# A gated cross-attention and feed-forward network on one core: the fusing stage and the last feed-forward stage as one pipeline

## The chip, the core and the metric

The kernel runs on one core of a Trainium2 chip. The time is that of the device, in microseconds (us), from launch to end, as the median of several executions. The core has five engines that run their own instruction lists: TensorE (PE, matrix products into the eight PSUM banks; its weight loads are shown apart as PEld), VectorE (DVE), ScalarE (ACT), GpSimd (POOL) and SyncE (SP, which here only issues transfers). They meet at semaphores. An engine executes its list in order, so whatever stands behind a wait waits too.

## The reference

The input `x` has 8 batches of 512 tokens with 512 values. Four layers follow one another, each added to `x` with a gate: attention over a context of 77 tokens, a mixture of experts (each token goes to its best two of eight, and to two shared ones), attention over the same context without projections, and a quantised feed-forward network with a convolution along the tokens. Only the last two and the end of the second concern us:

```python
routed_out = einsum('etd,te->td', routed, gates)          # two experts a token
x = x + tanh(g_ffn[0]) * (routed_out + shared_out)
# layer 3
h = layernorm(x)
p = softmax(h @ ctx.T)                                     # 77 scores a token
x = x + tanh(g_xattn[1]) * (p @ ctx)
# layer 4
h = layernorm(x)
h = quant(h) @ quant(w1).T                                 # 512 -> 2048, int8 per token
h = silu(conv3(h along the tokens) + conv_b)
x = x + tanh(g_ffn[1]) * (quant(h) @ quant(w2).T)          # 2048 -> 512
```

`quant` of an activation takes the largest absolute value of each token, scales to 127 and rounds.

## The kernel before

`flamingo` calls four stages: `attention`, `experts`, `fuse` and `ffn`. Each is a block of its own: no engine starts the next one before all have ended the last. The first two are not touched. A token tile is 128 tokens; a batch is four of them.

`fuse` (L1360) takes one batch a step, with three batches under way (`front`, `mid`, `back`). SP loads the residual rows `x2`; POOL gathers the two expert rows of each token by indirect transfers (L1517), eight a batch. DVE adds them with their gates (L1606, L1613) and takes the statistics (L1589, L1595), POOL the reciprocal root (L1525), ScalarE normalises (L1580). TensorE transposes (L1684), computes the scores (L1691), transposes the probabilities (L1695) and multiplies with the context (L1701); ScalarE copies and takes exponentials (L1568), DVE adds the result (L1661) and takes statistics again (L1666). The last third normalises (L1563), takes row maxima (L1633), quantises (L1576) and dequantises (L1601). The rows `x3` and `xd` go to DRAM (L1494, L1499). POOL loads the 4 MB `w1q` and the 2 MB `w2q` while this runs (L1532, L1533). The steady steps are a hardware loop.

`ffn` (L1706) loads `xd` and `x3` again. Its step also has three batches under way. TensorE transposes `xd` (L2033), ScalarE and DVE keep the result as a high and a low half (L1871, L1917). Then come the 16 up-projection tiles of 128 hidden values (L1988, eight matmuls each) through a ring of three PSUM banks `f_ps`. For each tile ScalarE writes the middle tap of the convolution into `h` (L1854), DVE adds the outer two (L1890, L1893), ScalarE applies the silu (L1836). DVE takes the maxima of eight tiles at a time (L1901), TensorE transposes them (L1998), DVE computes the token scales (L1906 to L1913), TensorE spreads them (L2004), ScalarE copies the row `srow` (L1847). For the batch before, POOL multiplies each tile with it (L1826; DVE does this for the last batch, L1936) and ScalarE rounds ("lifts") two tiles in each of slots 6 to 13 (L1841). For the batch before that, TensorE runs the down-projection one token tile at a time, sixteen matmuls and one for the offset (L1963, L1965): two token tiles at the start of the step, one behind up tile 5, one behind up tile 11. DVE adds the result to `x3` (L1883), and it goes out (L1803). `h` has three buffers. The last down-projection (L1976) runs through four banks at once, part by part behind the liftings.

## Time and profile before

| | |
|---|---|
| median of 3 runs | 1919.27 us (1912.75 to 1922.49) |
| profiled execution, its own time | 1918.68 us |
| its span, first to last instruction | 1917.2 us |
| mean granted TensorE clock | 0.904 |
| PE busy | 1653.6 us (86%), 8636 instructions |
| DVE busy | 1137.7 us (59%), 1946 instructions |
| ACT busy | 794.9 us (41%), 1417 instructions |
| POOL busy | 588.0 us (31%), 541 instructions |

Busy is the share of the span in which an engine executes something; waits, branches and the issuing of transfers don't count. The shares are averages over stages that differ. The activity strip cuts the span in 40 slices of 48 us and gives each a digit in tenths. `fuse` is slices 26 to 30, where PE drops to 3 to 7 and its clock to 5 to 7; `ffn` is the rest:

```profile
PE   7599999999866999998999999837674889999997
DVE  3587878878745344532223333258875777777775
ACT  2243433434313422222334443325563556566653
POOL 0133323333212444464331000065513243344440
PEclk9798989889967999999999999957666899999999
```

### The profile page before, as it was taken

How to read it: one execution, taken by the hardware profiler on the slowest of the kernel's cores; microseconds unless marked ns; L12 is line 12 of the kernel's file. 1: busy time of each engine (PE TensorE's matmuls, PEld its weight loads, DVE VectorE, ACT ScalarE, POOL GpSimd, SP SyncE). 2: the span in 40 equal slices, each digit the busy share in tenths (PEclk: the TensorE clock that was granted, in tenths of full speed). 3: DMA queues.
4: the chain of work that ended last, by engine and by line, in shares of the span. 5: the costliest groups of instructions: out<-in, count | busy, mean ns of one | idle time of the engine just before them, and what ended most of it. 6: DMA issues, size and time to landing. Idle time of an engine off the chain costs nothing. (4 is left out here: it accounts for less than half of the span.)

```text
span 1917.2 us, 26044 instructions
## 1 busy us (share of the span) xinstructions
PE 1653.6 (86%) x8636; PEld 1304.5 (68%) x8636; DVE 1137.7 (59%) x1946; ACT 794.9 (41%) x1417; POOL 588.0 (31%) x541
## 2 busy tenths in 40 slices
PE   7599999999866999998999999837674889999997
PEld 5578888788745888886778888624343666666664
DVE  3587878878745344532223333258875777777775
ACT  2243433434313422222334443325563556566653
POOL 0133323333212444464331000065513243344440
PEclk9798989889967999999999999957666899999999
DMA  3112122121129889984443333287743111111102
GB/s 124 44 45 88 55 77 88 44 88 55 67 74 351 286 304 316 321 282 138 162 139 107 107 108 106 94 303 287 256 148 110 44 44 66 66 66 38 51 23 88
DMA packets 108196, 252.02 MB, mean 131 GB/s; under 512 B 15027, under 2 KB 15027, under 8 KB 103912
## 3 DMA queue, kind: packets, MB, share of 16 engines
q1 hardware_dynamic: 65272, 121.98, 19.0%
q0 software_dynamic: 17056, 67.12, 9.7%
q10 hardware_dynamic: 25808, 62.14, 9.2%
q8 instruction: 35, 0.57, 0.1%
q14 instruction: 25, 0.20, 0.0%
HBM read 147.13 MB, written 101.97 MB: 130 GB/s over the span
## 5 line engine op out<-in xcount | busy, mean ns | idle before, releaser
L1275 PE MATMUL e_u_ps<-e_w,e_xeT 128*128 128x512 f32 x1596 | 393.1, 398 | 10.8 <-DVE e_xeT L1180 10.8
L1275 PEld LDWEIGHTS e_u_ps<-e_w,e_xeT 128*128 128x128 f32 x1596 | 293.1, 189 | 73.3 <-DVE e_w L1229 8.9
L1988 PE MATMUL b_f_ps<-b_xdT,w1q 128*128 128x512 f32 x1024 | 254.1, 404 | 11.5 <-DVE b_h L1893 9.4
L1988 PEld LDWEIGHTS b_f_ps<-b_xdT,w1q 128*128 128x128 f32 x1024 | 191.4, 190 | 64.8 <-DVE b_h L1893 18.3
L1826 POOL TENSOR_TENSOR b_h<-b_h,b_srow 128x512 f32<-128x512 f32 x112 | 143.6, 1342 | 245.9 <-ACT b_srow L1847 245.9
L1286 PE MATMUL e_y_ps<-e_w,e_hT 128*128 128x512 f32 x798 | 209.9, 405 | 4.3 <-DVE e_hT L1211 2.8
L1286 PEld LDWEIGHTS e_y_ps<-e_w,e_hT 128*128 128x128 f32 x798 | 143.3, 190 | 31.0 <-issue 4.0
L1854 ACT ACTIVATE b_h<-b_f_ps,cb,cw 128x512 f32<-128x512 f32 x128 | 104.2, 814 | 124.5 <-PE b_f_ps L1988 124.3
L1890 DVE SCALAR_TENSOR_TENSOR b_h<-b_f_ps,cw,b_h 128x511 f32<-128x511 f32 x128 | 95.9, 749 | 85.9 <-ACT b_h L1854 85.7
L490 ACT ACTIVATE pT<-t_ps 77x512 f32<-77x512 f32 x128 | 71.9, 590 | 119.0 <-PE t_ps L691 119.0
L465 POOL TENSOR_TENSOR prob<-prob,ri 128x1232 f32<-128x1232 f32 x32 | 74.9, 2341 | 115.3 <-DVE ri L572 115.3
L1211 DVE TENSOR_TENSOR e_hT<-e_h_ps,e_hT 128x256 fp32r<-128x256 f32 x69 | 29.3, 424 | 134.8 <-ACT e_hT L1046 134.8
L1965 PE MATMUL b_o_ps<-w2q,b_h 128*128 128x512 bf16 x448 | 106.2, 392 | 0.0
L730 PE MATMUL m_ps<-wo,oT 128*128 128x512 f32 x384 | 96.3, 407 | 7.1 <-DVE oT L598 7.0
L744 PE MATMUL m_ps<-xT,wq 128*128 128x256 f32 x768 | 98.3, 289 | 1.4 <-DVE xT L554 1.4
L1836 ACT ACTIVATE b_h<-b_h 128x512 f32<-128x512 f32 x128 | 86.7, 677 | 30.8 <-DVE b_h L1893 30.8
L1893 DVE SCALAR_TENSOR_TENSOR b_h<-b_f_ps,cw,b_h 128x511 f32<-128x511 f32 x128 | 96.2, 752 | 4.5
L691 PE MATMUL t_ps<-ident,prob 128*77 128x128 f32 x512 | 90.8, 340 | 7.6 <-ACT pT L490 4.9
L744 PEld LDWEIGHTS m_ps<-xT,wq 128*128 128x128 f32 x768 | 95.4, 196 | 1.8 <-DVE xT L554 1.8
L442 POOL TENSOR_TENSOR ve<-mv,eps 128x2 f32<-128x2 f32 x32 | 6.2, 194 | 289.6 <-DVE mv L583 289.6
L730 PEld LDWEIGHTS m_ps<-wo,oT 128*128 128x128 f32 x384 | 73.0, 194 | 27.9 <-DVE oT L598 11.5
L985 POOL DMA_INDIRECT slots_in_scratch<-e_srow,e_scol x64 | 71.8, 1122 | 56.7 <-DMA e_srow<-xn_scratch 37.3
(221 smaller groups left out, 2869.1 us busy)
## 6 DMA issues: line engine op xcount, KB each, us to landing
e_xe<-slots_in_scratch SPq DMA_DIRECT2D x69, 256.0 KB, 2.6
experts_out_scratch<-e_ye ACTq DMA_DIRECT2D x69, 256.0 KB, 2.0
xin<-in_x SPq DMA_DIRECT2D x16, 512.0 KB, 3.8
xres<-in_x SPq DMA_DIRECT2D x16, 512.0 KB, 4.5
x_scratch<-x SPq DMA_DIRECT2D x32, 256.0 KB, 2.1
xn_scratch<-xn SPq DMA_DIRECT2D x32, 256.0 KB, 2.1
e_xe<-xn_scratch SPq DMA_DIRECT2D x32, 256.0 KB, 4.2
e_fraw<-in_w1T ACTq DMA_DIRECT2D x8, 1024.0 KB, 8.3
```

Of the source, the lines that this page charges most:

```text
L691: mm = pe.transpose(t_ps[0:C, t[("p", j, g)] % 2, i * P:(i + 1) * P], prob[:, j, g * HG + i, :], ident[:])
L730: mm = pe.matmul(m_ps[:, m[f"w{j}"] % 2], oT[:, pa, k, j * P:(j + 1) * P], wo[:, pb, k, :], start=(k == 0 and (pa, pb) == PASSES[0]), stop ...
L744: mm = pe.matmul(m_ps[:, m[f"q{i}"] % 2, g * W2:(g + 1) * W2], wq[:, pa, k, mt * P:(mt + 1) * P], xT[:, pb, k, :], start=(k == 0 and (pa, ...
L1275: mm = pe.matmul(u_ps[:, i], xeT[:, pa, k], w[:, par, pb, k * 2 * HID:(k + 1) * 2 * HID], start=(k == 0 and (pa, pb) == PASSES[0]), stop=( ...
L1286: mm = pe.matmul(y_ps[:], hT[:, pa, i * KH + k], w[:, par, pb, W1N + k * D:W1N + (k + 1) * D], start=(i == 0 and k == 0 and (pa, pb) == PA ...
L1826: pool.tensor_tensor(ht, ht, srow[:], ALU.mult).then_inc(u_done, 1)
L1836: act.activation(ht, ht, ACT.Silu).then_inc(h_done, 1)
L1854: act.activation(tile(s, m), f_ps[:, (s * KF + m) % RING], ACT.Identity, bias=cb[:, m:m + 1], scale=cw[:, m, 1:2]).then_inc(mid_tap, 1)
L1890: dve.scalar_tensor_tensor(out=ht[:, 1:S], in0=f[:, 0:S - 1], scalar=cw[:, m, 0:1], in1=ht[:, 1:S], op0=ALU.mult, op1=ALU.add).then_inc(pr ...
L1893: dve.scalar_tensor_tensor(out=ht[:, 0:S - 1], in0=f[:, 1:S], scalar=cw[:, m, 2:3], in1=ht[:, 0:S - 1], op0=ALU.mult, op1=ALU.add).then_in ...
L1965: mm = pe.matmul(o_ps[:, j % 2], rounded(s - 2, k, j), w2q[:, k, :], start=False, stop=(k == KF - 1))
L1988: mm = pe.matmul(f_ps[:, u % RING], w1q[:, k, m * P:(m + 1) * P], xdT[:, part, k], start=(k == 0 and part == 0), stop=(k == KD - 1 and par ...
```

## The change

`fuse` and `ffn` become one block, `tail`, whose steps run over `s` from -2 to 9, each written out as slots `m` = 0 to 15. In step `s` the expert rows of batch `s+2` are combined (`comb_next`), batch `s+1` goes through cross-attention and quantising (`cross`), batch `s` through the up-projection (`up`), the hidden values of batch `s-1` get their token scales (`quant`), and batch `s-2` goes through the down-projection (`down`). There is no hardware loop.

- `x3` and `xd` no longer go through DRAM; the rows of a batch stay in one of five buffers `X` from load to output.
- ScalarE multiplies the gathered rows with their gates (`gate_experts`, slots 1, 2, 9, 10) and POOL adds them, where DVE did both. The gathers take their indices straight from `slot`; `y` has four row buffers, and each pair of gathers is issued behind the additions that free its buffers.
- The down-projection works on all four token tiles at once, in four banks of its own (`y_ps`): part `m` follows up tile `m` in each slot. DVE's four outputs come together at the end of the step.
- Everything else on TensorE shares one ring of four banks, `r_ps`, in written order (`ring`): up tiles, transposes, scores, probabilities, maxima, scale row, attention. A use waits for the last reader of the use four before it.
- `h` has two buffers instead of three; a middle tap waits for the down-projection part that frees its tile (`h_free`). ScalarE lifts one tile a slot: tiles 7 to 15 of batch `s-2` in slots 0 to 8, tiles 0 to 6 of batch `s-1` in slots 9 to 15.
- `w1q` is loaded behind the first four gathers, `w2q` on SP's queue.

```diff
-        n.w1q = keep("w1q", [P, KD, DH], FR)
...
-        fuse(nc, n)
-        ffn(nc, n)
+        tail(nc, n)
...
+        r_ps = psum("r_ps", [P, RING, 512])
+        y_ps = psum("y_ps", [P, TB, D])
...
+            for s in range(-2, B + 2):
+                run(s, 0 <= s - 2, 0 <= s - 1 < B, 0 <= s < B, 0 <= s + 1 < B, s + 2 < B)
+
+        ring = []
+        for s in range(-2, B + 1):
+            for m in range(KF):
+                if 0 <= s < B:
+                    ring.append(("f", s, m))
+                if 0 <= s + 1 < B:
+                    if m < 2:
+                        ring += [("x", s + 1, 2 * m), ("x", s + 1, 2 * m + 1)]
+                    if m == 2:
+                        ring.append(("s", s + 1, 0))
+                    if m == 4:
+                        ring.append(("p", s + 1, 0))
+                if 1 <= s <= B:
+                    if m == 4:
+                        ring += [("a", s - 1, 0), ("a", s - 1, 1)]
+                    if m == 6:
+                        ring.append(("r", s - 1, 0))
+                if 0 <= s + 1 < B and m in (7, 8):
+                    ring += [("o", s + 1, 2 * m - 14), ("o", s + 1, 2 * m - 13)]
+            if 0 <= s + 1 < B:
+                ring += [("d", s + 1, j) for j in range(TB)]
...
@@ GpSimd, one step @@
+                if 2 <= s <= B:
+                    products(s - 2, 7, KF)
+                if comb_next:
+                    combine(s + 2, 0)
+                    combine(s + 2, 1)
+                if quant and up:
+                    pool.wait_ge(row_done, s)
+                    products(s - 1, 0, 2)
+                if cross:
+                    rstd(1, mv2_done, s + 1, nmr2_done)
+                if quant and up:
+                    products(s - 1, 2, 4)
+                if comb_next:
+                    combine(s + 2, 2)
+                    combine(s + 2, 3)
+                if quant and up:
+                    products(s - 1, 4, 7)
+                if comb_next:
+                    rstd(0, mv1_done, s + 2, nmr1_done)
...
@@ ScalarE, in slot m @@
+                    if up:
+                        if s >= HB:
+                            act.wait_ge(h_free, (s - HB) * KF + m + 1)
                         act.wait_ge(f_full, s * KF + m + 1)
...
+                    if 2 <= s <= B and m < 9:
+                        lift_tile(s - 2, 7 + m)
+                    if quant and up and m >= 9:
+                        lift_tile(s - 1, m - 9)
+                    if comb_next and m in (1, 2, 9, 10):
+                        gate_experts(m - 1 if m < 3 else m - 7)
...
@@ VectorE, in slot m and behind the slots @@
+                    if up:
                         taps(m)
...
+                    if quant and m == 5:
+                        token_scales()
+                    if cross and m in (8, 9):
+                        fused(2 * m - 16)
+                        fused(2 * m - 15)
+                    if cross and m == 9:
+                        aggregate(1, stats[0] - TB, mv2_done)
+                    if up and m == 10:
+                        half_max(0)
...
+                if quant and not up:
                     dve.wait_ge(row_done, s)
                     for m in range(KF):
...
                         dve.tensor_tensor(ht, ht, srow[:], ALU.mult).then_inc(u_done, 1)
...
+                if down and not up:
+                    for j in range(TB):
+                        outputs(j)
...
@@ TensorE, in slot m @@
+                    if up:
+                        up_tile(m)
+                    if down and m >= 1:
+                        down_part(m)
+                    if cross and m < 2:
+                        normed_transposes(2 * m)
+                        normed_transposes(2 * m + 1)
+                    if down and m == 0:
+                        down_part(0)
+                    if cross and m == 2:
+                        scores(0)
+                        scores(1)
+                    if cross and m == 4:
+                        prob_transposes()
+                    if quant and m == 4:
+                        max_transposes(0)
+                        max_transposes(1)
+                    if quant and m == 6:
+                        scale_row()
+                    if cross and m in (7, 8):
+                        attend(2 * m - 14)
+                        attend(2 * m - 13)
+                if cross:
+                    for j in range(TB):
+                        quantised_transposes(j)
```

## Rows read from the trace of the kernel before

**Rows 1.** Windows: stretch, its length, busy us of PE, PEld, DVE, ACT, POOL, clock, DMA.
```profile
1244.40:1457.80 213.40, 121.20 (x480) 78.00 (x480) 155.88 (x368) 101.26 (x201) 88.39 (x111) 0.63 0.68 238
1457.80:1469.80 12.00, 3.67 (x16) 3.27 (x16) 2.76 (x4) 2.39 (x4) 11.92 (x3) 0.54 0.32 91
...
1877.40:1917.20 39.80, 29.56 (x136) 15.88 (x134) 21.36 (x30) 11.09 (x18) 0.00 (x0) 0.90 0.22 79
```

**Rows 2.** Chain that ended last, up tiles 2 to 5 of two batches: start, us, what.
```profile
1675.65 7.47 PE b_f_ps L1988 x32
...
1838.65 7.46 PE b_f_ps L1988 x32
```

**Rows 3.** Timeline of `ffn`: start, us, engine, line, operation, tiles, count, idle before.
```profile
1670.80 3.96 PE L1988 MATMUL b_f_ps<-b_xdT,w1q 128*128 128x512 f32 x16
...
1672.99 0.80 ACT L1854 ACTIVATE b_h<-b_f_ps,cb,cw 128x512 f32<-128x512 f32 x1 [10.30 <-PE b_f_ps L1988]
...
1675.38 7.30 PEld L1988 LDWEIGHTS b_f_ps<-b_xdT,w1q 128*128 128x128 f32 x32
...
1682.97 3.35 PEld L1965 LDWEIGHTS b_o_ps<-w2q,b_h 128*128 128x128 f16 x16
```

**Rows 4.** Timeline of `ffn`, ScalarE and DVE at slots 7 to 9.
```profile
1688.70 0.82 ACT L1854 ACTIVATE b_h<-b_f_ps,cb,cw 128x512 f32<-128x512 f32 x1 [4.14 <-PE b_f_ps L1988]
1689.55 0.76 DVE L1890 SCALAR_TENSOR_TENSOR b_h<-b_f_ps,cw,b_h 128x511 f32<-128x511 f32 x1 [4.00 <-ACT b_h L1854]
...
1691.13 0.80 ACT L1854 ACTIVATE b_h<-b_f_ps,cb,cw 128x512 f32<-128x512 f32 x1
...
1698.21 4.41 DVE L1901 TENSOR_REDUCE b_am<-b_h 128x512 f32<-128x4096 f32 x1
```

**Rows 5.** POOL: the products in the timeline, the gathers in the groups by line.
```profile
1679.47 20.53 POOL L1826 TENSOR_TENSOR b_h<-b_h,b_srow 128x512 f32<-128x512 f32 x16 [34.23 <-ACT b_srow L1847]
...
L1517 POOL DMA_INDIRECT y<-experts_out_scratch,ycol x64 | 64.0, 999 | 23.7 <-issue 16.7 <-POOL ycol L1513 6.7 <-DVE f_mv L1595 0.3
```

**Rows 6.** Groups by line in `fuse`: busy us, mean ns of one, idle before.
```profile
L1701 PE MATMUL f_o_ps<-f_craw,prT 77*128 77x512 f32 x64 | 57.0, 1071 | 5.5 <-ACT prT L1571 5.5
L1691 PE MATMUL f_s_ps<-f_ctraw,f_xT 128*128 128x77 f32 x256 | 30.9, 281 | 0.0
```

**Rows 7.** Timeline of `fuse`, the first batches and the last.
```profile
1270.52 0.16 DVE L1649 SCALAR_TENSOR_TENSOR nmr<-f_mv,f_rs 128x4 f32<-128x4 f32 x1 [1.45 <-POOL f_rs L1525]
...
1276.86 1.28 ACT L1568 ACT_TABLE_LOAD   x1
...
1291.86 0.41 DVE L1595 BATCH_NORM_AGGREGATE f_mv<-f_st 128x2 f32<-128x6 f32 x4
...
1295.77 2.93 ACT L1563 ACTIVATE xq<-x,nmr,f_rs 128x512 f32<-128x512 f32 x4 [1.14 <-DVE nmr L1626]
...
1298.22 2.45 DVE L1633 TENSOR_REDUCE am<-xq 128x1 f32<-128x512 f32 x4
...
1304.76 2.54 ACT L1576 ACTIVATE xq<-xq,sc 128x512 f32<-128x512 f32 x4
...
1445.65 2.93 ACT L1563 ACTIVATE xq<-x,nmr,f_rs 128x512 f32<-128x512 f32 x4 [8.51 <-DVE nmr L1626]
```

**Rows 8.** Transfers of `fuse`: issues, KB each, median us to landing.
```profile
w1q<-w1q_scratch POOLq DMA_DIRECT2D x1, 4096.0 KB, 15.1
...
y<-experts_out_scratch,ycol POOLq DMA_INDIRECT x64, 6.3
```

**Rows 9.** Timeline of the end: DVE's products for the last batch.
```profile
1888.35 2.50 DVE L1936 TENSOR_TENSOR b_h<-b_h,b_srow 128x512 f32<-128x512 f32 x4 [2.79 <-ACT b_srow L1847]
```

**Rows 10.** Windows in `ffn`, as rows 1: TensorE's clock around two pauses.
```profile
1508.00:1512.00 4.00, 0.45 (x2) 0.45 (x3) 4.00 (x2) 0.00 (x0) 0.00 (x0) 0.50 0.93 284
1512.00:1516.00 4.00, 4.00 (x14) 3.27 (x13) 3.06 (x8) 0.00 (x0) 0.00 (x0) 0.50 0.64 241
...
1660.00:1662.00 2.00, 2.00 (x12) 1.94 (x11) 1.21 (x2) 1.84 (x4) 0.00 (x0) 0.52 0.00 0
```

More of the change, by code:

```diff
@@ L1933, in run @@
+                if comb_next:
+                    combined(2)
+                    combined(3)
+                    aggregate(0, stats[0] - TB, mv1_done)
+                if cross:
+                    for j in range(TB):
+                        low(j)
+                if down and up:
+                    for j in range(TB):
+                        outputs(j)
+                if up:
+                    half_max(1)
+                if quant and not up:
                     dve.wait_ge(row_done, s)
@@ L2040 @@
+                if cross:
+                    for j in range(TB):
+                        quantised_transposes(j)
+            whole(run)
 def kernel(x, ctx_1024, g_xattn, g_ffn, L0_xattn_Wq, L0_xattn_bq, L0_xattn_Wk, L0_xattn_bk, L0_xattn_Wv,
```

848 lines of the change are left out of this document (359 added, 489 removed).

## Prediction, made before the changed kernel ran

> **What bounds the kernel now.** I read the activity strip of the page first, then windows by stage, then the timeline inside the last two stages. The change touches only what comes after the expert stage, from 1244.4 us on. There the fusing stage takes 213.4 us with TensorE granted 0.63 of its clock and busy 121 us; DVE, at 156 us, is its busiest engine [rows 1]. A hand-over of 12.0 us follows (a block boundary, the first load of `xd`, its transposes), then the feed-forward stage, and 39.8 us from its last convolution to the end [rows 1]. In the steady feed-forward stage one batch takes (1838.65 - 1675.65)/3 = 54.3 us [rows 2]. A batch of the fusing stage takes about 22 us (from 1295.77, the second normalisation of the first batch, to that of the eighth at 1445.65 it is 7 x 21.4 [rows 7]). So a batch costs some 76 us in both stages together.
>
> In the feed-forward stage TensorE is the bound. An up-projection tile is eight matmuls at 0.229 us from start to start (7.30 us for 32), 1.8 us; a down-projection matmul is 0.213 us (3.35 us for 16) [rows 3]. One batch is 16 x 1.8 + 68 x 0.213 = 43.5 us, and with 16 + 16 transpose-like instructions and the four sets of `xd` transposes about 48 of the 54.3 us. The first matmul of a tile starts at 1670.80 and ScalarE's reading of it at 1672.99: 2.2 us, that is 0.4 us behind the last matmul [rows 3].
>
> **The prices of the other engines.** Between two middle taps ScalarE does a silu and two liftings, four instructions in 1691.13 - 1688.70 = 2.43 us, about 0.6 us each. A tile's two outer taps are 2 x 0.76 = 1.5 us of DVE, and half of a batch's maximum 4.4 us [rows 4]. A product on POOL is 20.53/16 = 1.28 us, a gather 80.7/64 = 1.26 us (busy and issue) [rows 5]. Four normalisations are 2.9 us, four quantisations 2.5 us, four row maxima 2.5 us [rows 7].
>
> **The sum of one full slot sequence (batches 2 to 5), engine by engine.**
> - TensorE: 48 us as above, plus 16 transposes (2.7 us), scores (32 instructions of about 0.1 us, 3.2), transposes of the probabilities (0.6) and attention. An attention instruction runs 0.89 us (57.0/64) at a clock of 0.63, about 0.45 us at the full one, and a batch has 8 of them: 3.6 us [rows 6]. Together 58 us.
> - DVE: 16 x 1.5 + 2 x 4.4 + outputs 2.8 + low halves 2.5 + token scales 2.1 + attention's four outputs with their statistics 5.8 + statistics of the combined rows 2.5 + row maxima 2.5 + dequantising 1.7 + some small ones 2.5 = 55 us. The two combining passes have left DVE.
> - ScalarE: 48 tile instructions at about 0.6 (30), two normalisations (5.8), quantising (2.5), eight gatings (4.9), eight copies (4.3), exponentials (1.3), and two table loads of 1.28 each, because each batch now has its exponentials between silus (the trace has the load where the first exponential follows the experts' silus [rows 7]): 52 us.
> - POOL: 16 products (20.5), 8 additions for combining (10.3, priced as products), 8 gathers (10), two reciprocal roots (3.6): 44 us.
>
> No engine needs more than 58 us. If only the busiest counted, the stage would shrink from 76 to some 60 us a batch. I don't forecast that, because all three engines must pass each tile on in turn through one ring of four PSUM banks, which now carries the cross-attention's tiles too.
>
> **The wait structure, slot by slot.** Time 0 is the end of DVE's last taps of the step before. "Mid m" is the start of ScalarE's middle tap of tile m; it now waits for the down-projection part that frees the buffer (two `h` buffers, not three): tile start + 1.8 + 0.86 + 0.4 = 3.1 us.
> - Boundary: low halves end at 4.2, outputs at 7.0, the second maximum at 11.3; down part 0 waits for the outputs. Mid 0 at 9.5, taps 0 from 11.3 to 12.8. The third transpose set waits for taps 0. Mid 1 is at 12.2, mid 2 at 17.1.
> - Scores stand ahead of tile 3 on TensorE: mid 3 at 23.0. Table load, exponentials, a lifting: mid 4 at 27.4; second load, silu.
> - Tile 5 takes the bank of tile 4 (three maxima and probability banks lie between): it starts when taps 4 end at 29.7, mid 5 at 32.8. Tile 6 takes the bank of the probabilities (copied at 34.6): mid 6 at 37.6. Tile 7 stands behind the scale row, which waits for token scales behind taps 5: mid 7 at 41.4. Tile 8 takes the scale row's bank (43.2): mid 8 at 46.2.
> - Attention output 3 and tile 9 wait for DVE's fused rows 0 and 1 (49.2, 50.6): mid 9 at 53.6. Taps 9, fused rows 2 and 3, aggregate: 59.1.
> - Then DVE: taps 10, maximum, taps 11, statistics, taps 12, row maxima and scales until 72.1.
> - POOL starts its root at 59.1: 1.8, products 2 and 3 (2.6), two combinings with two gathers behind each (2 x 5.4), product 4: 75.6. ScalarE's lifting of that tile stands ahead of quantising, which thus runs 76.2 to 78.6 and not 72.1 to 74.6. Mid 14 at 78.6, taps 14, dequantising, taps 15 end at 84.
>
> So 84 us a full step, against 76: each slot from 4 to 9 is a chain over three engines of 4 to 7 us.
>
> **The sum.** From 1244.4. The first batch's rows are ready at 1270.5 now [rows 7]. In the new order the 4 MB load of `w1q` is issued behind the first four gathers and ahead of the next four, on the same queue; it took 15.1 us to land [rows 8]. If the gathers wait for it the rows are ready at 1285, if not at 1278; I take 1281. Cross-attention of batch 0, nothing beside it: now 1270.5 to 1292.3 for the fused rows and statistics [rows 7], then root, normalisation, maxima, quantising, dequantising, transposes, copies, 11 us: 33 us, 1314. Step 0 (no down-projection, no products): the same chain, 61 us, 1375. Step 1 (no outputs, no down parts): 84 - 9 = 75, 1450. Steps 2 to 5: 4 x 84 = 336, 1786. Step 6 (nothing to combine, quantising at once): 78, 1864. Step 7 (no cross-attention): taps 0 at 11.3, then TensorE, 16 x 2.7: 53, 1917. The end: outputs and maximum 7.1, transposes, scales and row 5.8, 16 products at 0.625 (2.50 for 4 [rows 9]) 10, then DVE's outputs of batch 6 (2.8), and only behind them the whole down-projection of batch 7, 68 x 0.213 = 14.7, outputs 2.8 and the last transfer 4.8: 48, against 39.8 now [rows 1]. Today that down-projection runs beside the liftings. 1965, and with the 1.5 us between span (1917.2) and time (1918.68): 1966. The profiled execution is 0.6 us under the median.
>
> **Two prices weighed.** A switch of ScalarE's table is 1.28 us in the trace [rows 7], and I use that. The Trainium skill (ScalarE: Activation LUTs, What ACT_TABLE_LOAD costs) adds a drain and puts a switch at 2.66 us; by that figure a full step would be an estimated 2.8 us longer and the time 1984 us. No row here shows such a drain.
>
> TensorE's clock: with TensorE nearly idle from 1508 to 1512 the granted clock is 0.50, the lower level of 1.2 GHz, and it stays there from 1512 to 1516 with TensorE busy all 4.00 us; behind the pause from 1656 on it is 0.52 in 1660 to 1662 [rows 10]. By my schedule TensorE idles some 10 us in each full step, from the last down part to the dequantised rows, so tile 0 takes 3.6 us, not 1.8, and taps 0 start about 1 us later, since DVE's maximum covers the rest. I price it at 0 to 1 us a step (in the 84). The Trainium skill (TensorE: Matmul & The Clock Gate, HAM oscillation) says that matmul groups separated by idle time keep falling back to half rate; the row agrees, and this is the third rival's mechanism.
>
> **Rivals.**
> 1. Faster: the overlap works and the busiest engine bounds. Today's feed-forward step is 54.3 for 48 us of its bound, 1.13; 58 x 1.13 = 65. Then steps 2 to 5 lose 19 us each, 0, 1 and 6 some 32 in all: 1966 - 108 = 1858. For it: no engine is over 58 us, and two stages' idle time lies open to each other. Against it: bank and order waits above. It decides from 77 us a full step: seven steps of cross-attention at 7 us less win back the 47 us. Between (about 77): 1919.
> 2. Late gathers: from issue to landing a gather takes 6.3 us [rows 8]; POOL issues those of the next pair only behind each combining. Should a pair land after ScalarE reaches slot 9, gating waits with the tiles of slots 9 and 10 behind it, about 3 us a step: 1966 + 6 x 3 = 1984. Against it: by my times 14 us or more lie between issue and gating.
> 3. Slower still: the clock stays at its lower level through slots 3 to 9, where TensorE works in pieces of 2.7 us between waits. Six tiles and their down parts at double time, less what is hidden: 6 to 8 us a step for six steps: 2005 to 2010. Against it: in those slots my pauses are 1 to 3 us, shorter than the two above behind which the clock fell.
>
> **How the numbers follow.** A measurement tells 0.5% (10 us) from no change. Forecast, steps of 79 to 88 us: 0.44, between 1940 and 1990. Rival 2: 0.06. Rival 3: 0.12. Rival 1: 0.26. Between, steps near 77: 0.12, of which 0.05 faster, 0.07 same. Faster 0.31, same 0.07, slower 0.62. The range 1880 to 2005 leaves out most of rival 1 and the far end of rival 3; the forecast's own range is 1940 to 1990.
>
> **What would show it.** Full steps of 84 us from one table load pair to the next; DVE idle for ScalarE in slots 3 to 9; ScalarE waiting for POOL's product ahead of quantising; TensorE's tile 5 and 9 released by DVE; 16 table loads; a last down-projection that starts only behind DVE's outputs. If DVE or TensorE is busy over 80% between 1450 and 1786, the forecast is wrong, and if the steps are under 77 us its sign is.

## The result, and the profile after

The changed kernel takes 2014.37 us (1999.44 to 2017.20), the kernel before, in the same comparison, 1920.05 us: 1.048 times as long, interval 1.042 to 1.054. The forecast was 1966 us, its range 1880 to 2005. The sign was right, the size was not.

The profiled execution has a span of 2011.9 us (1917.2 before) at a mean clock of 0.895 (0.904). The first part of the page after; the activity strip is in 40 slices of 50 us:

```profile
PE 1665.0 (83%) x8636; PEld 1308.7 (65%) x8636; DVE 1101.6 (55%) x1874; ACT 850.9 (42%) x1495; POOL 669.3 (33%) x628
...
PE   7599999999849999999999996266676878787796
...
PEclk9798898898769999999999998578888979797899
...
HBM read 130.36 MB, written 85.20 MB: 107 GB/s over the span
```

Against the kernel before, VectorE has 36 us less to do, ScalarE 56 and GpSimd 81 us more, as the change moved it, and 33.5 MB of transfers are gone (147.13 MB read and 101.97 written before). Yet PE is at 6 to 8 tenths from the first up tile on, but for one 9 near the end, where the old feed-forward stage had 8s and 9s. Windows of the kernel after (length; busy us of PE, PEld, DVE, ACT, POOL; clock), which answer to [rows 1]: the start, steps 1 to 3, and from the last taps to the end:

```profile
1244.40:1325.00 80.60, 19.10 (x76) 13.34 (x76) 21.76 (x46) 26.43 (x46) 45.01 (x49) 0.54 0.54 187
1385.00:1465.00 80.00, 52.99 (x220) 39.65 (x220) 50.85 (x81) 46.53 (x79) 30.32 (x31) 0.80 0.15 43
1465.00:1556.40 91.40, 69.19 (x300) 47.27 (x300) 53.72 (x87) 53.74 (x92) 41.80 (x40) 0.85 0.10 27
1556.40:1645.50 89.10, 67.24 (x289) 45.70 (x288) 53.45 (x85) 52.49 (x89) 41.77 (x40) 0.84 0.17 51
...
1961.70:2011.90 50.20, 34.92 (x152) 17.58 (x152) 24.30 (x37) 15.96 (x27) 0.00 (x0) 0.90 0.17 63
```

DVE's 53, ACT's 53 and POOL's 42 us a step are close to the forecast's 55, 52 and 44. TensorE's 67 to 69 are not its 58, since it ran at 0.85 of its clock. The step is 20 us longer than that.

The forecast's terms against the trace, a step counted from one last tap of DVE to the next:

| term | forecast | measured | difference |
|---|---|---|---|
| first up tile starts | 1314 | 1326.3 | +12.3 |
| step 0 | 61 | 61.4 | +0.4 |
| step 1 | 75 | 80.1 | +5.1 |
| steps 2 to 5 | 336 | 88.5 + 89.1 + 88.5 + 84.9 = 351.0 | +15.0 |
| step 6 | 78 | 86.2 | +8.2 |
| step 7 (no cross-attention) | 53 | 57.0 | +4.0 |
| the end | 48 | 49.9 | +1.9 |

Together 46.9 us, which is the whole miss of the profiled execution. Step 3 on TensorE (start, us, what; in brackets the idle time before and its releaser):

```profile
1560.29 3.78 PE L1914 MATMUL t_r_ps<-t_xdT,t_w1q 128*128 128x512 f32 x8 [2.71 <-DVE t_xdT L1816]
...
1586.97 2.13 PE L1914 MATMUL t_r_ps<-t_xdT,t_w1q 128*128 128x512 f32 x8 [1.29 <-DVE t_h L1774]
...
1591.89 3.23 PE L1914 MATMUL t_r_ps<-t_xdT,t_w1q 128*128 128x512 f32 x8 [1.90 <-ACT t_prT L1702]
1594.93 1.56 PE L1897 MATMUL t_y_ps<-t_w2q,t_h 128*128 128x512 bf16 x4
...
1597.13 2.10 PE L1914 MATMUL t_r_ps<-t_xdT,t_w1q 128*128 128x512 f32 x8
...
1608.30 1.10 PE L1962 MATMUL t_r_ps<-t_craw,t_prT 77*128 77x512 f32 x2 [2.36 <-DVE t_x L1790]
1609.58 3.69 PE L1914 MATMUL t_r_ps<-t_xdT,t_w1q 128*128 128x512 f32 x8 [0.19 <-DVE t_x L1790]
...
1642.88 3.38 PE L1968 MATMUL t_r_ps<-ident,t_xw 128*128 128x128 f32 x14 [11.49 <-DVE t_xw L1850]
```

Tile 5 waits for the taps of tile 4, tile 6 for the copy of the probabilities, tile 9 stands behind the attention output that waits for DVE's fused row: the bank waits as forecast. Not forecast is the length of tiles 6 and 9: 3.2 and 3.7 us, where tile 7 takes 2.1. Windows of the same stretch:

```profile
1590.00:1592.00 2.00, 0.11 (x1) 0.11 (x1) 1.02 (x2) 1.97 (x4) 0.00 (x0) 1.00 0.00 0
1592.00:1594.00 2.00, 2.00 (x6) 1.60 (x7) 1.93 (x5) 0.44 (x1) 0.00 (x0) 0.64 0.01 4
1594.00:1596.00 2.00, 2.00 (x6) 0.80 (x5) 0.45 (x4) 0.00 (x0) 0.00 (x0) 0.51 0.00 0
1596.00:1598.00 2.00, 2.00 (x15) 1.74 (x13) 0.63 (x1) 1.48 (x3) 0.00 (x0) 1.00 0.01 4
...
1610.00:1612.00 2.00, 2.00 (x6) 1.52 (x6) 0.26 (x1) 0.00 (x0) 0.00 (x0) 0.50 0.65 159
```

The granted clock went to its lower level (1.2 GHz) behind pauses of 1.90 and 2.36 us, and came back some 3 us later. Both falls stand in each of steps 2 to 6. The forecast had argued that pauses of 1 to 3 us would not do this.

The trace of the kernel before already had such a fall, at the start of a feed-forward step (TensorE, then the window; the clock had been 1.00 from 1712 to 1714):

```profile
1712.98 0.66 PE L2033 MATMUL b_f_ps<-ident,b_xd 128*128 128x128 f32 x4 [2.18 <-DVE b_h L1893]
1714.42 1.76 PE L2033 MATMUL b_f_ps<-ident,b_xd 128*128 128x128 f32 x8 [0.79 <-DVE b_h L1893]
...
1716.00:1718.00 2.00, 2.00 (x6) 0.74 (x5) 2.00 (x2) 1.01 (x3) 0.00 (x0) 0.50 0.36 38
```

Nor does the length of a pause alone tell. In step 0 of the changed kernel pauses of 2.24 and 2.35 us brought no fall (1.00 from 1342 to 1348 and from 1355 to 1361). e6_lock, a kernel of the experiments below, is the same program as the changed one up to step 6, and in its step 2 tile 6 comes behind the same pause at the full clock:

```profile
1500.72 2.13 PE L1916 MATMUL t_r_ps<-t_xdT,t_w1q 128*128 128x512 f32 x8 [1.91 <-ACT t_prT L1704]
```

ScalarE's lifting waits for POOL's product 4 and quantising stands behind it, as forecast:

```profile
1637.06 0.67 ACT L1652 ACTIVATE t_h<-t_h 128x512 f32<-128x512 f32 x1 [6.83 <-POOL t_h L1606]
1637.63 2.54 ACT L1717 ACTIVATE t_xw<-t_xw,t_sc 128x512 f32<-128x512 f32 x4
```

The start: POOL's list has its product with the convolution's constants ahead of the first combining. Their transfers run beside the 4 MB of `w1q`; the second of them, 8 KB, landed 18.5 us after it was issued (time and bracket as before):

```profile
1265.00 0.42 POOL L1637 TENSOR_SCALAR t_cw<-t_cw,mean 128x48 f32<-128x48 f32 x1 [14.86 <-DMA t_cb<-in_conv_b]
```

### The profile page after: what moved, and what is told of

Read it like the earlier page. It is cut to its first block and busy times, and to the rows that moved or that the text cites. A ratio compares the mean times of both kernels' runs of the same rounds, so it can differ in the third digit from the quotient of the medians.

```text
span 2011.9 us, 25959 instructions
## 1 busy us (share of the span) xinstructions
PE 1665.0 (83%) x8636; PEld 1308.7 (65%) x8636; DVE 1101.6 (55%) x1874; ACT 850.9 (42%) x1495; POOL 669.3 (33%) x628
## 5 line engine op out<-in xcount | busy, mean ns | idle before, releaser
L1914 PE MATMUL t_r_ps<-t_xdT,t_w1q 128*128 128x512 f32 x1024 | 299.6, 441 | 49.9 <-DVE t_xdT L1816 20.6
L1914 PEld LDWEIGHTS t_r_ps<-t_xdT,t_w1q 128*128 128x128 f32 x1024 | 204.0, 205 | 119.3 <-DVE t_xdT L1816 23.8
L1771 DVE SCALAR_TENSOR_TENSOR t_h<-t_r_ps,t_cw,t_h 128x511 f32<-128x511 f32 x128 | 95.6, 747 | 225.4 <-ACT t_h L1685 225.2
L1606 POOL TENSOR_TENSOR t_h<-t_h,t_srow 128x512 f32<-128x512 f32 x112 | 142.7, 1316 | 147.3 <-ACT t_srow L1658 147.2
L1685 ACT ACTIVATE t_h<-t_r_ps,t_cb,t_cw 128x512 f32<-128x512 f32 x128 | 103.8, 811 | 183.4 <-PE t_y_ps L1897 151.0
L1897 PE MATMUL t_y_ps<-t_w2q,t_h 128*128 128x512 bf16 x512 | 134.8, 396 | 0.0
L1968 PE MATMUL t_r_ps<-ident,t_xw 128*128 128x128 f32 x128 | 30.6, 426 | 84.3 <-DVE t_xw L1850 84.3
L1652 ACT ACTIVATE t_h<-t_h 128x512 f32<-128x512 f32 x128 | 84.6, 678 | 35.7 <-POOL t_h L1606 35.0
L1774 DVE SCALAR_TENSOR_TENSOR t_h<-t_r_ps,t_cw,t_h 128x511 f32<-128x511 f32 x128 | 96.2, 752 | 4.5
L1647 ACT ACTIVATE t_h<-t_h 128x512 f32<-128x512 f32 x128 | 85.6, 669 | 22.1 <-DVE t_h L1774 21.9
```

What stands on the lines that cost most here:

```text
L1606: pool.tensor_tensor(ht, ht, srow[:], ALU.mult).then_inc(u_done, 1)
L1647: act.activation(ht, ht, ACT.Silu).then_inc(h_done, 1)
L1685: act.activation(tile(s, m), bank("f", s, m), ACT.Identity, bias=cb[:, m:m + 1], scale=cw[:, m, 1:2]).then_inc(mid_tap, 1)
L1771: dve.scalar_tensor_tensor(out=ht[:, 1:S], in0=f[:, 0:S - 1], scalar=cw[:, m, 0:1], in1=ht[:, 1:S], op0=ALU.mult, op1=ALU.add).then_inc(pr ...
L1774: dve.scalar_tensor_tensor(out=ht[:, 0:S - 1], in0=f[:, 1:S], scalar=cw[:, m, 2:3], in1=ht[:, 0:S - 1], op0=ALU.mult, op1=ALU.add).then_in ...
L1897: mm = pe.matmul(y_ps[:, j], rounded(s - 2, k, j), w2q[:, k, :], start=False, stop=(k == KF - 1))
```

## The experiments

Times are medians; "ratio" is against runs of the kernel before on the same chip (1919.6 to 1925.9 us, by chip). "Step" is the mean of steps 2 to 5, from one second half maximum of DVE to the next, in the profiled execution: 88.4 us in the changed kernel. Two kernels whose order in these steps is the changed kernel's, e4_prologue and e6_lock, have 88.0. The rows come from several chips, so a difference of two medians is less sure than one of two ratios. The kernel before has 54.3 + 21.4 = 75.7 us for the same work in its two stages [rows 2, 7].

| run | us | ratio (95%) | clock | step |
|---|---|---|---|---|
| the changed kernel | 2014.4 | 1.048 (1.042, 1.054) | 0.895 | 88.4 |
| e1_warm | 1989.5 | 1.032 (1.027, 1.037) | 0.921 | 85.2 |
| e2_down_first | 1999.6 | 1.040 (1.036, 1.045) | 0.907 | 85.4 |
| e3_pool_order | 1990.4 | 1.032 (1.025, 1.038) | 0.906 | 83.1 |
| e4_prologue | 2000.0 | 1.039 (1.034, 1.043) | 0.896 | 88.0 |
| e5_all | 1955.5 | 1.015 (1.012, 1.018) | 0.930 | 79.3 |
| e6_lock | 2007.9 | 1.046 (1.041, 1.052) | 0.899 | 88.0 |
| e7_tables | 1986.4 | 1.029 (1.025, 1.034) | 0.902 | 84.8 |
| e8_two_banks | 1964.4 | 1.022 (1.016, 1.028) | 0.905 | 80.1 |
| e9_all_end | 1951.2 | 1.011 (1.006, 1.016) | 0.925 | 79.5 |
| e10_ring_order | 1946.7 | 1.014 (1.009, 1.018) | 0.903 | 77.8 |
| e11_row_order | 2002.8 | 1.044 (1.040, 1.049) | 0.900 | 86.1 |
| e12_all_orders | 1909.0 | 0.998 (0.994, 1.001) | 0.932 | 75.1 |
| e13_rows_sooner | 1917.8 | 0.999 (0.997, 1.001) | 0.920 | 75.5 |
| e14_no_filler | 1913.7 | 0.996 (0.994, 0.998) | 0.908 | 74.6 |
| e15_ring_both | 1925.0 | 1.002 (1.000, 1.004) | 0.905 | 74.4 |
| e16_few_fillers | 1916.5 | 0.997 (0.995, 1.000) | 0.920 | 75.7 |
| e17_orders_only | 1913.6 | 0.997 (0.994, 0.999) | 0.914 | 75.3 |

### Four single causes

```diff
@@ e1_warm: TensorE, ahead of tile 6 (6), attention output 3 (8), the quantised transposes (24 or 36) @@
+    pe.matmul(acc, lift[:], zero[:, 0:1].to_broadcast([P, 512]), start=first, stop=first)   # adds zeros
@@ e2_down_first: TensorE, in slot m @@
-    if up: up_tile(m)
     if down and m >= 1: down_part(m)
+    if up: up_tile(m)
@@ e3_pool_order: GpSimd @@
-    products(s - 1, 2, 4)
+    products(s - 1, 2, 7)
     combine(s + 2, 2); combine(s + 2, 3)
-    products(s - 1, 4, 7)
@@ e4_prologue: GpSimd, from ahead of all steps to behind the first batch's combining @@
+    if s == -2: (load of w1q, wait for the constants, their two products)
```

What was expected of the four, in this order, before they ran:

> Adds matmuls that change nothing (zeros accumulated into an open bank, or written to a bank that the quantised transposes overwrite) into TensorE's pauses: 6 ahead of tile 6, 8 ahead of attention output 3, 36 between the last down part and the quantised transposes, in each step with cross-attention. Theory (clock): TensorE falls to its lower level behind these three pauses and pays 1.6 us at tile 6, 1.6 us at tile 9 and about 1 us at the transposes: full steps go from 88.4 to about 84 us, the kernel 25 to 30 us down, to about 1985 us. Rival (the clock is covered by other waits; the steps are long because of order and banks alone): below 8 us.

> In each slot from 1 on the down-projection part is issued ahead of the up tile instead of behind it, so that it runs while TensorE waits for the tile's bank, and the middle tap waits 0.86 us less. Theory (banks and order): in slots 5, 6, 8 and 9 a chain over three engines loses 0.86 us each, and with the shorter pauses the clock may hold: 3.4 to 6.5 us a full step, 20 to 35 us in all, to 1980 to 1992 us. Rival (the busiest engine's work bounds the step, order does not matter): no change within 5 us.

> GpSimd does products 2 to 6 together ahead of the two combinings and their gathers, instead of 2 and 3 before and 4 to 6 behind them. Theory: ScalarE's lifting of tile 4, which stands ahead of quantising, no longer waits 6.8 us; steps 2 to 5 get 4 to 5 us shorter, the kernel about 18 us, to about 1995 us. Rival (that wait is covered, the step's end is set by VectorE): within 5 us.

> The 4 MB load of w1q, the wait for the convolution's constants and their scaling on GpSimd move behind the combining of batch 0. Theory: the first combining waits for the constants (14.9 us idle), whose transfer shares the DMA engines with w1q; the first up tile starts at about 1314 instead of 1326.3, the kernel 10 to 13 us down. Rival: w1q then lands too late for tile 0, no gain.

The fillers took 3.2 us off a step. In the same step of that kernel tile 6 takes 2.12 us instead of 3.23, since its pause of 1.90 us holds 1.47 us of fillers:

```profile
1580.19 1.47 PE L1925 MATMUL t_y_ps<-t_zero,t_lift 128*128 128x512 bf16 x6
1582.26 2.12 PE L1919 MATMUL t_r_ps<-t_xdT,t_w1q 128*128 128x512 f32 x8 [0.60 <-ACT t_prT L1705]
```

So the lower clock was a price here. With the down part ahead of its tile (e2) a step was 3.0 us shorter, under the 3.4 to 6.5 expected, and the time, 1999.6, stayed above the expected 1980 to 1992. With POOL's new order (e3) a step was 5.3 us shorter, the most of the four: quantising no longer waits for the two combinings. The prologue moved the first up tile from 1326.3 to 1316.4. That start is less sure than its time suggests: without the edit the profiled kernels of this study have it anywhere from 1313.3 to 1330.8, with it from 1303.4 to 1317.3, so some 13 us between the means of the two groups (10 kernels and 8).

These gains are not each the edit's own. The fall of the clock ahead of tile 6 went away in e2, in steps 3 to 5 of e3, and in e7 and most steps of e11 below, which were not made for it. Step 2, from last taps to last taps, with the lengths of three up tiles, tells the two apart (us):

| run | step 2 | tile 0 | tile 6 | tile 9 |
|---|---|---|---|---|
| the changed kernel | 88.5 | 2.71 | 2.93 | 3.45 |
| e3_pool_order | 83.5 | 2.71 | 2.92 | 3.48 |
| e6_lock (same order in this step) | 86.8 | 3.56 | 2.13 | 3.27 |
| e4_prologue (same order in this step) | 86.6 | 3.51 | 2.13 | 3.31 |
| e1_warm | 86.1 | 3.78 | 2.13 | 2.13 |
| e2_down_first | 86.4 | 3.54 | 2.13 | 3.87 |
| e7_tables | 85.0 | 3.52 | 2.13 | 3.27 |
| e11_row_order | 85.4 | 3.43 | 2.13 | 3.40 |

With tile 6 slow on both sides, POOL's order is worth 5.0 us. The fall ahead of tile 6 alone costs 1.8 us here (88.5 against 86.7); between steps 3 and 4 of e11_row_order, without and with it, lie 3.2 us. Each row is one execution. With tile 6 fast on both sides, the down part first is worth 0.3 us, against 3.0 by the mean of the steps: most of what e2 gave is the clock, which its expectation had named as a possibility.

> The three edits of the runs before in one kernel: filler matmuls in TensorE's pauses (3 ahead of tile 6, 8 ahead of the third attention output, 24 or 36 ahead of the quantised transposes) together with the down part ahead of the up tile in each slot, POOL's products 2 to 6 ahead of the two later combinings, and w1q and the constants loaded after the first batch's combining. Alone they took 31, 32 and 18 us off the changed kernel. Theory 1, separate causes (the clock in the pauses, the wait of ScalarE's lifts for POOL, the late first rows): the gains add up, middle steps about 80 us (88.4 - 3 - 5), the time 1930 to 1945, ratio about 1.01. Theory 2, one slack: the early slots wait on one chain and each edit only cuts another piece of the same wait, so the best of them is nearly all there is: middle steps 82 to 83 us, the time 1965 to 1980.

e5_all has all four edits (3 fillers ahead of tile 6 instead of 6). A step is 79.3 us, 9.1 us shorter; the three gains add up to 11.5. The 2.4 us between are of the size of the fall ahead of tile 6, which each of the three single runs had counted (e3 in three of its four steps). So the steps are as theory 1 had them (about 80), with in the main two causes in them: the clock and POOL's order. The time, 1955.5 us, lies in neither theory's range (1930 to 1945, 1965 to 1980); the ratio left is 1.015.

### POOL's elementwise work and VectorE's

```diff
@@ GpSimd @@
+    if s == B - 1:
+        pool.wait_ge(xdt_lo, B * TB)
     if 2 <= s <= B:
         products(s - 2, 7, KF)
```

What was expected before it ran:

> One wait added, on POOL in the seventh step alone: it starts that step's nine products only when the quantised rows of the step before are all written, so POOL is idle while VectorE computes step 6's row scales (in the changed kernel it ran 14 products back to back there, 17.76 us, and three tensor_scalar instructions of 4 elements took 0.74, 1.12 and 1.33 us). Theory 1, POOL's elementwise instructions slow VectorE's: the three are 0.17 to 0.25 us each. Rival, VectorE waits there for something else that the profile puts into the instruction: they keep 0.7 to 1.3 us. The step's length (86.0 us) may fall by 2 to 3 us or be eaten by the later products; it is not what this run is for.

Two timelines, first of the changed kernel's step 6 (POOL, then DVE), then of e6_lock's:

```profile
1884.32 16.50 POOL L1606 TENSOR_TENSOR t_h<-t_h,t_srow 128x512 f32<-128x512 f32 x13
...
1893.86 0.74 DVE L1807 TENSOR_SCALAR t_ax<-t_ax 128x4 f32<-128x4 f32 x1
1894.72 1.12 DVE L1810 TENSOR_SCALAR t_dq<-t_ax 128x4 f32<-128x4 f32 x1
1895.76 1.33 DVE L1812 TENSOR_SCALAR t_sc<-t_axi 128x4 f32<-128x4 f32 x1
```

```profile
1890.48 0.17 DVE L1809 TENSOR_SCALAR t_ax<-t_ax 128x4 f32<-128x4 f32 x1
...
1890.77 0.14 DVE L1812 TENSOR_SCALAR t_dq<-t_ax 128x4 f32<-128x4 f32 x1
1890.89 0.17 DVE L1814 TENSOR_SCALAR t_sc<-t_axi 128x4 f32<-128x4 f32 x1
```

Theory 1 held: 3.19 us of DVE became 0.48, and the step 83.3 us instead of 86.0.

The same effect stands in other runs, and in the steady steps too. In the changed kernel the first of the three takes 0.79 to 0.81 us in each of steps 1 to 4. In e10_ring_order and e15_ring_both, described below, one of them takes 4.4 us in each of steps 2 to 4, until POOL is done (e10_ring_order, step 3):

```profile
1594.20 4.38 DVE L1810 TENSOR_SCALAR t_dq<-t_ax 128x4 f32<-128x4 f32 x1
1594.77 3.77 POOL L1606 TENSOR_TENSOR t_h<-t_h,t_srow 128x512 f32<-128x512 f32 x3
```

ScalarE's quantising then waits 1.92 us for the last of the three. In e12_all_orders, e16_few_fillers and e17_orders_only one takes 1.8 and another 1.2 us in each of steps 2 to 4, and in step 6 of the last two one takes 7.5 us. In step 6 of e1_warm, e4_prologue and e7_tables one takes 8.2 us, so their times show less than their edits gave. No run took this out of a steady step.

### The tables

```diff
-    act.activation(pr[:, j], ..., ACT.Exp, bias=nm[:, j:j + 1], accum_out=su[:, j:j + 1])
+    act.activation(pr[:, j], ..., ACT.Silu, bias=nm[:, j:j + 1], accum_out=su[:, j:j + 1])
```

What was expected before it ran:

> The softmax's exponential is computed as a Silu (its output is left out of the reference's arithmetic), so ScalarE needs no table switch in the steps. Theory 1, a table load costs what its row shows, 1.28 us twice a step, beside the chain that ScalarE's mid taps feed: the eight steps with cross-attention are together 10 to 20 us shorter. Rival, a load also drains the engine behind the row, 2.66 us a switch (the Trainium skill, ScalarE's page on table loading): 35 to 42 us. Second rival, ScalarE's time has slack where the loads fall: under 6 us.

A step is 3.6 us shorter, against 2 x 1.28 = 2.57 by the rows (`L1696 ACT ACT_TABLE_LOAD x8 | 10.3, 1283 | 0.1` in the changed kernel). From the first tile to the last maximum the profiled execution gained 13.8 us; its step 6 was 2.2 us longer, for a reason found by accident: one instruction of DVE took 8.22 us while POOL ran its products.

```profile
1867.98 17.74 POOL L1606 TENSOR_TENSOR t_h<-t_h,t_srow 128x512 f32<-128x512 f32 x14
...
1877.52 8.22 DVE L1807 TENSOR_SCALAR t_ax<-t_ax 128x4 f32<-128x4 f32 x1
```

But the 3.6 us are not the loads' alone. In steps 2 to 6 of e7_tables tile 6 takes 2.12 to 2.14 us, so the clock's fall ahead of it is gone too. Against the kernels in which it is also gone in step 2 (table above), the step is 1.7 us shorter: within the rows' 2.57, and far from the rival's 5.3 (2 x 2.66). The medians differ by 28 us, between theory 1 and the rival; they hold the clock too and are no evidence for a drain. By the step, none shows.

### The ring of four banks

```diff
@@ e8_two_banks: token tiles j and j + 2 of the down-projection are summed in one bank @@
-    RING = 4
+    RING = 6
-        y_ps = psum("y_ps", [P, TB, D])
+        y_ps = psum("y_ps", [P, 2, D])
@@ e10_ring_order: VectorE, in slot m @@
+    if quant and m == 5: token_scales()
+    if cross and m in (8, 9): fused(2 * m - 16); fused(2 * m - 15)
+    if cross and m == 9: aggregate(...)
     if up: taps(m)
     ...
-    (the same three, behind the taps)
@@ e10_ring_order: TensorE and the ring's order, slot 4 @@
+    max_transposes(0); max_transposes(1)
     prob_transposes()
-    max_transposes(0); max_transposes(1)
```

What was expected of the two, and of both together, before they ran:

> The down-projection accumulates its four token tiles in two PSUM banks instead of four (tiles 0 and 2 share one, 1 and 3 the other, so the results are sums of pairs and the output is not the reference's), and the ring for up tiles and cross-attention has six banks instead of four; instructions, operands and counts on every engine are the same. Theory 1, the four-bank ring delays the up tiles by the fusing tiles put into it: a middle step loses 4 to 6 us, the time falls by 20 to 35 us. Rival, the ring is not what the tiles wait for, since each slot waits for ScalarE's and VectorE's own order: 0 to 1 us a step, the time within 8 us of the changed kernel's.

> The changed kernel with three moves and nothing else: VectorE adds the attention outputs 0 and 1 before the taps of slot 8 instead of after them, 2 and 3 before those of slot 9, and reads the token maxima before the taps of slot 5; TensorE transposes the probabilities after the maxima instead of ahead of them. Each frees banks of the ring of four earlier. Theory 1 (two more banks took 7 us off a middle step): the ring binds through late readers, and earlier readers give back 3 to 5 us a step, the time falls by 20 to 35 us. Rival, only more banks help, since TensorE must run ahead of ScalarE's round trip: 0 to 1.5 us a step, under 10 us.

> The changed kernel with the earlier readers (1947 us) and also six banks in the ring, the down-projection's token tiles summed in pairs in two banks (the output is not the reference's). Theory 1, the two edits removed the same wait, and the ring no longer binds: within 8 us of 1947. Rival, the ring still binds after the reordering: 10 to 30 us less, middle steps 75 to 77 instead of 78.9.

Both worked beyond their expectations: 50 us for two more banks, 68 us for moves that change no instruction, only the order. A part of both is the clock: steps 2 to 5 of these two have no fall ahead of tile 6 or 9, and that was worth 3.2 us a step in e1_warm. TensorE's idle time by releaser over steps 1 to 5 (us in total, times, longest), first the changed kernel, then e10_ring_order:

```profile
PE t_r_ps L1968 <- DVE t_xw L1850: 55.6, 5, 13.8
...
PE t_r_ps L1962 <- DVE t_x L1790: 11.8, 5, 2.4
PE t_r_ps L1914 <- ACT t_prT L1702: 9.5, 5, 1.9
```

```profile
PE t_r_ps L1968 <- DVE t_xw L1850: 45.4, 5, 10.6
...
PE t_r_ps L1914 <- DVE t_h L1774: 10.1, 6, 2.0
```

The waits for the fused rows and for the copied probabilities are gone; tiles 8 and 9 of e10_ring_order start 4.2 us apart, not 7.5, and take 2.1 and 2.4 us, at a granted clock of 1.00 from 1561 to 1579:

```profile
1570.11 2.14 PE L1914 MATMUL t_r_ps<-t_xdT,t_w1q 128*128 128x512 f32 x8 [0.20 <-ACT t_srow L1658]
...
1574.30 2.43 PE L1914 MATMUL t_r_ps<-t_xdT,t_w1q 128*128 128x512 f32 x8
```

DVE in step 3 of the changed kernel shows what the move uses. Attention outputs 0 and 1 were done at 1601.9; DVE idled 3.41 us ahead of taps 8 and fused the first of them only behind these, and idled 4.80 us ahead of taps 9 in the same way. TensorE waited 2.36 us for the first of these banks:

```profile
1605.96 0.75 DVE L1771 SCALAR_TENSOR_TENSOR t_h<-t_r_ps,t_cw,t_h 128x511 f32<-128x511 f32 x1 [3.41 <-ACT t_h L1685]
...
1607.41 0.74 DVE L1790 SCALAR_TENSOR_TENSOR t_x<-t_r_ps,t_rt,t_x 128x512 f32<-128x512 f32 x1
```

Which of the three moves brought how much was not taken apart. With both edits (e15_ring_both) another 22 us went, and the step is 74.4 us: the rival, the ring still binds after the reordering.

### The chain of the rows

```diff
@@ e11_row_order: VectorE @@
+    if cross and m == 12: row_max(0..3); row_scales()
+    if cross and m == 14: (the four dequantising instructions)
     if up: taps(m)
     ...
-    (both, behind the taps)
```

What was expected before it ran:

> The changed kernel with two moves on VectorE: the row maxima and scales ahead of the taps of slot 12, and the product with the quantised rows ahead of the taps of slot 14. Theory 1, the end of a step is the chain of the rows (statistics, normalise, maxima, scales, quantise, transposes, subtraction), and TensorE idles 11.5 us ahead of the quantised transposes: the chain is 2.5 to 4 us shorter a step, the time falls by 18 to 30 us. Rival, the chain waits for ScalarE's lifts and POOL's products whatever VectorE does, and the taps become late in its place: 0 to 1 us a step.

The step lost 2.3 us and the time 11.6, between theory and rival. Much of it is the clock again. In steps 2, 3 and 5 tile 6 came at the full clock (2.12 to 2.13 us) and the steps lost 3.1, 3.7 and 2.4 us; in step 4 it did not (2.77 us), and the step is as long as the changed kernel's (88.6 and 88.5). Against e4_prologue and e6_lock in step 2 the moves are worth 1.3 us. ScalarE's quantising stands behind a lifting that waits for POOL, so VectorE's half alone is worth little.

### All together, and what is left of the fillers

```diff
@@ e9_all_end: e5_all, and VectorE in the last-but-one step @@
     for m in range(KF): (product m)
+        if m == 3: outputs(0..3)
-    outputs(0..3)
@@ e12_all_orders: e9_all_end + e10_ring_order + e11_row_order, less the 8 fillers in slot 8 @@
@@ e13_rows_sooner: e12, row steps a slot earlier on ACT and DVE, 12 fillers at the step's end @@
@@ e14_no_filler: e13 without fillers.  e16_few_fillers: e12 with 12.  e17_orders_only: e12 with none @@
```

What was expected of e9_all_end before it ran:

> The kernel with the three edits together, and in the last-but-one step VectorE writes batch 6's outputs after 4 of its 16 products instead of after all 16. Theory 1, the last down-projection starts only behind these outputs: the stretch from the last taps to the end is 5 to 8 us shorter than that of the same kernel without this edit (about 50 us). Rival, the products and the lifts bound that stretch themselves: it moves by under 1 us.

From the last half maximum to the end of the span it was 45.1 us instead of 48.6 (e5_all) and 47.4 (changed kernel): 3.5 us, under theory 1's 5 to 8 but not the rival's 1.

Of the other five, in the order e12, e13, e14, e16 and e17:

> The kernel of the three edits with the earlier outputs at the end (1951 us), with both orders of this call, and without the 8 filler matmuls ahead of the third attention output. Theory 1, the kernel loses to the one before only by waits at hand-overs, not by work: middle steps 71 to 75 us (79.0 less 4 to 8), below the 76 of the kernel before, the time 1885 to 1925, at or under the kernel before. Rival, the step is bound by TensorE's 67 us at 0.85 of the clock and what must follow serially: 77 to 79 us a step, 1940 to 1950.

> The kernel with all orders (1909 us), with ScalarE's part of the rows' chain moved too: it normalises in slot 10 instead of 11 and quantises in slot 12 instead of 13, VectorE's maxima and scales stand ahead of the taps of slot 11, its product ahead of those of 13, the first half maximum in slot 12; and 12 filler matmuls instead of 36 ahead of the quantised transposes (there the fillers ended 3.5 us after the rows were ready). Theory 1, the rows' chain ends a step: middle steps 69 to 72 us instead of 74.9, the time 1875 to 1895, under the kernel before. Rival, the chain moves but the last taps bound the step: 73 to 75 us, 1900 to 1910.

> The same kernel without any filler matmul. Theory 1, the clock's price depends on the pauses that are left (about 8 us at a step's end, under 2 elsewhere): 1 to 2.5 us a step more than with fillers, 8 to 20 us in all. Rival, the clock was a follower, and no filler is needed once the waits are gone: within 4 us of it.

> The kernel of all orders (1909 us) with 12 filler matmuls instead of 24 or 36 ahead of the quantised transposes, nothing else. Theory 1, the step's end waited for the fillers (they ran from 1646.6 to 1654.5 us, the rows were ready at 1650.8): 2 to 3.5 us a step less, the time 1885 to 1895. Rival, the last taps and their banks bound the end, and the lower clock takes back what the fillers cost: within 6 us of 1909.

> The same without any filler. Theory 1, waits gone, the clock's price is under 1 us a step: within 6 us of the kernel with 12 fillers. Rival, the clock costs 2 us a step: 10 to 16 us above it.

e12_all_orders came out as theory 1 had it: the step is 75.1 us and the time that of the kernel before. After that nothing moved it. With the rows a slot earlier (e13) the step is 75.5 us and the time 1917.8: theory 1 (69 to 72 us) missed, and the rival (73 to 75 us, 1900 to 1910) came nearer. The quantised transposes then waited for banks that the last taps hold, as in e17_orders_only (first e13, then e17):

```profile
1648.88 1.08 PE L1983 MATMUL t_r_ps<-ident,t_xw 128*128 128x128 f32 x4 [2.07 <-DVE t_h L1777]
```

```profile
1650.54 1.73 PE L1983 MATMUL t_r_ps<-ident,t_xw 128*128 128x128 f32 x8 [5.03 <-DVE t_xw L1820]
1654.22 1.09 PE L1983 MATMUL t_r_ps<-ident,t_xw 128*128 128x128 f32 x4 [1.95 <-DVE t_h L1777]
```

Fewer fillers or none (e14, e16, e17): no difference, though the clock was 0.914 (e17) instead of 0.932 (e12). e16's theory 1 (1885 to 1895) missed: it took 1916.5 us. e14 came out 4.2 us under e13, and e17 2.9 us under e16. Once the mid-step pauses are gone, the clock that fillers keep is not on the path; what is lost behind the step's last pause lies beside DVE's maximum.

## Why the prediction was wrong

**The sum's work.** Right. DVE, ACT and POOL were within some 2 us of the list, and no engine bound the step; rival 1 (faster) needed that. Two slips in it cost nothing: attention's 0.89 us at a clock of 0.63 is 0.56 and not 0.45 at the full one (four such instructions took 1.88 us), and 68 x 0.213 is 14.5 and not 14.7.

**The slot waits.** Right in place, and the mechanism held: tiles 5, 6, 8 and 9 were released by the readers named, quantising stood behind POOL's product 4. Counted from the last taps of step 2, the middle taps 5 to 9 of step 3 came at 33.7, 40.2, 43.8, 48.8 and 57.9 us, forecast 32.8, 37.6, 41.4, 46.2 and 53.6. The 4.3 us that were missing at slot 9 stay to the end of the step (89.1, forecast 84).

**The clock.** This is the step that failed: "I price it at 0 to 1 us a step (in the 84)". The fillers of e1_warm, which do no work of the kernel, gave back 3.2 us a step, and the two slow tiles of step 3 with their down part are 1.1 + 0.5 + 1.6 = 3.2 us over their undisturbed lengths: most of the 3.8 us by which steps 2 to 5 were longer on average. The argument behind it ("my pauses are 1 to 3 us, shorter than the two above behind which the clock fell") read a threshold into two rows; the falls came behind pauses of 1.90 and 2.36 us, and the trace before had one behind 2.18 and 0.79 us. So rival 3's mechanism took place at some half of its size, in tiles 6 and 9 and not in all of slots 3 to 9. The range's upper end, 2005 us, had left out nearly all of that rival, to which the forecast gave 0.12. Over the whole kernel e1_warm took 25 us off by medians (31 by ratios), of a miss of 48; its profiled steps 1 to 6 are together 12.9 us shorter, with a stall of 8.21 us in step 6. The Trainium skill (TensorE: Matmul & The Clock Gate, A second HAM failure mode: psum-queue depth-cycling) tells of a kernel whose TensorE idles briefly between its matmul groups as it cycles through PSUM banks, and whose clock keeps falling and coming back; this trace agrees, with two falls in the middle of step 3.

**The start.** 12.3 us: the forecast knew of `w1q` ahead of the gathers, and not that POOL's own list has the product with the constants ahead of the first combining, 14.86 us of waiting. Every instruction of the moved step was to be counted, and this was one. Without that list's order changed, the first tile came anywhere from 1313.3 to 1330.8 us, so some of the 12.3 us is chance.

**Step 6.** 8.2 us. POOL's 14 products back to back held up VectorE's scales, 2.7 us (e6_lock). The two falls of the clock stand in this step as in the others; the rest was not taken apart. Nothing in the profile before shows POOL's effect: there the same three instructions took 0.14 to 0.24 us in every batch.

**The table loads.** 16, each 1.28 us with its neighbours adjacent, as used. Taking them out made a step 3.6 us shorter, and 1.7 us where the clock did the same on both sides; the forecast's 2.57 us, without a drain, was enough.

**The gathers** (rival 2) were not late where the forecast looked: no gating of slots 9 and 10 in step 3 shows a wait for them.

**Steps 1 and 7** were 5.1 and 4.0 us longer than forecast. In step 1 of the changed kernel tiles 5 and 6 ran at the lower clock (3.78 us each); in e6_lock, the same program, they did not (2.13) and the step was 1.5 us shorter. The rest was not taken apart.

**The reading of the whole.** The forecast took the four-bank ring's waits as given by the design, and they were given by the order of a few instructions. No single term makes the miss: the clock in each of steps 1 to 6, the start and POOL's effect in step 6 are its named parts. Every term of the sum came out too small, so no error hid another. Of the 94 us that the change cost, moves alone took away all: e17_orders_only, the changed kernel in another order and without any filler, runs at 0.997 of the kernel before (0.994 to 0.999), e12_all_orders at 1909 us (0.998, with an interval that holds 1). That is under the 0.5% taken here as no change. The pipeline as such, in the orders tried, is then worth about nothing: its step is 75 us, as the two stages' 75.7. Not all of that is its floor: e17_orders_only still has instructions of VectorE that take 1.8 and 1.2 us beside POOL in each of steps 2 to 4, and 7.47 us in step 6. No run removed these, so what they cost is open.

## What to carry to other kernels

When work is put beside a tight hand-over loop on shared buffers, don't sum the engines: write down for each buffer who reads it last and what stands ahead of that reader in its own list. A reader that has its input and stands behind an instruction still waiting is the first thing to move, and it can be worth more than two more buffers. Price the clock for every pause of a step, not only the longest, and look in the trace before for falls behind short pauses. On every moved list count the small instructions that wait for transfers. When single edits are compared, check whether they removed the same wait: here a fall of the clock that went away without being aimed at was part of four gains (e2, e3, e7, e11).

## What was not expected of the hardware

An elementwise instruction of VectorE on 128x4 values took 0.74 to 8.22 us instead of 0.14 to 0.17 while POOL ran `tensor_tensor` back to back, up to six of POOL's 1.28 us products. The reciprocal between them kept its 0.18 us and VectorE's taps, which read PSUM, their 0.75. It went away where POOL was made idle (step 6 of e6_lock), and stayed in that run's steps 1 to 4 (0.80 to 0.84). The Trainium skill (SBUF — State Buffer, Who interferes with whom) says that VectorE in a two-port mode and GpSimd share a port pair, which one holds for a whole instruction while the other fully blocks; the trace agrees in kind, and shows that the wait can last over several of POOL's instructions.

TensorE's granted clock fell to its lower level behind pauses of 1.90 and 2.36 us and stood at full again some 3 us later. Behind the same pause of 1.9 us ahead of tile 6 it fell in some steps and held in others, of the same program even.
